# Two turns in a row, then the expert products of two tiles, with four places for their halves

## The reference, cut to what matters

```python
h = _swiglu(flat @ w1.T)
routed = jnp.zeros_like(shared)
for e in range(NUM_EXPERTS):
    routed = routed + h * w_se[:, e:e + 1] @ w2[e].T
return (shared + routed).reshape(Bs, Ts, C)
```

## Time and profile before

| | us |
|---|---|
| median of three executions | 1170.11 |
| lowest and highest | 1168.33, 1171.01 |
| the profiled execution | 1173.07 |
| its span, from the first to the last instruction | 1171.4 |
| TensorE busy in the span | 1107.7 (95%) |
| VectorE busy | 809.8 (69%) |
| GpSimd busy | 521.6 (45%) |
| ScalarE busy | 474.3 (40%) |

### The profile page before, as it was taken

How to read it: one execution, slowest core, us unless ns; L and a number is a source line. 1 busy time by engine, 2 the same in 40 slices (tenths; PEclk the granted TensorE clock), 3 DMA queues, 4 the chain that set the end, 5 groups by cost and what they waited for, 6 DMA issues and landing times.

```text
span 1171.4 us, 22483 instructions
## 1 busy us (share of the span) xinstructions
PE 1107.7 (95%) x7475; PEld 919.2 (78%) x7475; DVE 809.8 (69%) x1778; ACT 474.3 (40%) x723; POOL 521.6 (45%) x647
## 2 busy tenths in 40 slices
PE   3678999999999999999999899999999899999997
PEld 2456878887888788787787677788888788888886
DVE  6555687787686786876877676557554588777776
ACT  5454555555556545555555442223222111111111
POOL 6223446457447447356455522200000566666664
PEclk8887999999999999999999999999999899999999
DMA  8886566657647656665754411577662454545452
GB/s 154 219 135 125 114 107 134 131 92 148 137 103 126 131 119 102 144 131 114 125 118 88 90 40 43 172 243 257 213 207 100 150 159 152 164 159 155 152 162 73
DMA packets 106163, 160.65 MB, mean 137 GB/s; under 512 B 28828, under 2 KB 70718, under 8 KB 106048
## 3 DMA queue, kind: packets, MB, share of 16 engines
q1 hardware_dynamic: 94276, 121.18, 46.0%
q0 software_dynamic: 11776, 38.03, 10.5%
HBM read 75.24 MB, written 52.10 MB: 109 GB/s over the span
## 4 chain that ended last, share of the span: by engine, by line
PE 73%; DVE 8%; issue 8%; POOL 5%; DMA 3%; ACT 2%; SPq 1%; POOLq 0%; ACTq 0%; DVEq 0%
PE ps L744 15%; PE ps L791 11%; PE ps L689 9%; PE ps L706 6%; PE ps L793 6%; PE ps L609 4%; PE ps L597 4%; PE ps L640 3%; PE ps L776 3%; PE ps L565 2%; PE ps L569 2%; POOL tab_dram L1455 2%; DMA regr<-regr 1%; PE ps L592 1%; PE ps L663 1%
## 5 line engine op out<-in xcount | busy, mean ns | idle before, releaser
L791 PE MATMUL ps<-regr,gh 128*128 x600 | 222.1, 407 | 0.5 <-issue 0.3
L873 ACT ACTIVATE Pt<-ps,pbias 77x1024 f32<-77x1024 f32 x128 | 141.8, 1108 | 108.8 <-PE ps L597 104.8
L793 PE MATMUL ps<-regr,gl 128*128 x600 | 170.2, 284 | 0.0
L791 PEld LDWEIGHTS ps<-regr,gh 128*128 128x128 f32 x600 | 114.0, 190 | 24.4 <-issue 1.1
L963 ACT ACTIVATE gh<-ps 128x512 fp32r<-128x512 f32 x75 | 44.8, 600 | 206.9 <-PE ps L776 102.3
L1173 DVE TENSOR_REDUCE mneg<-ps 128x8 f32<-128x616 f32 x128 | 101.2, 792 | 29.7 <-PE ps L569 29.6
L793 PEld LDWEIGHTS ps<-regr,gl 128*128 128x128 f32 x600 | 114.2, 190 | 0.0
L689 PE MATMUL ps<-x2h,winh 128*128 128x512 f32 x256 | 110.2, 430 | 0.6 <-DVE OHR L1078 0.6
L1431 POOL TENSOR_TENSOR x<-x,regf 128x512 f32<-128x512 f32 x32 | 41.1, 1284 | 154.8 <-DMA x<-in_x 154.8
L1356 POOL TENSOR_TENSOR gl<-gf,gh 128x512 fp32r<-128x512 f32 x64 | 82.5, 1289 | 44.7 <-ACT gh L830 44.5
L689 PE MATMUL ps<-x2h,winl 128*128 128x512 f32 x256 | 101.5, 397 | 0.0
(11 more groups left out here) (202 smaller groups left out, 2678.9 us busy)
## 6 DMA issues: line engine op xcount, KB each, us to landing
regr<-regr SPq DMA_DIRECT2D x96, 256.0 KB, 5.9
y_dram<-Pt SPq DMA_DIRECT2D x64, 256.0 KB, 2.2
regf<-in_x SPq DMA_DIRECT2D x32, 256.0 KB, 3.0
x<-in_x SPq DMA_DIRECT2D x32, 256.0 KB, 7.2
y_dram<-res SPq DMA_DIRECT2D x32, 256.0 KB
regr<-regr SPq DMA_DIRECT2D x96, 77.0 KB, 6.9
x_dram<-x2h SPq DMA_DIRECT2D x14, 512.0 KB, 3.0
x_dram<-x2l SPq DMA_DIRECT2D x14, 512.0 KB, 3.8
```

The lines of the kernel that those rows point to most:

```text
L791: e.matmul(o, gh2[:, k % 3, fc, :], w2v[:, bass.ds(val, 1), fc, :, :].rearrange("p o h d -> p (o h) d"), start=fc == 0, stop=False, skip_g ...
L793: m = e.matmul(o[:, 0, :], gl2[:, k % 3, fc, :], w2v[:, bass.ds(val, 1), fc, 0, :].rearrange("p o d -> p (o d)"), start=False, stop=fc == ...
L873: e.activation(Pt[0:K, 4 * k:4 * k + 4, :].rearrange("k (n j) t -> k n (j t)", n=2), bank_of["sc", b, k][0:K, :, :], ACT.Exp, bias=pbias[: ...
```

## The change

`gh2` and `gl2` get four places instead of three (`k % 4`); ScalarE's wait for a free place moves by one tile with it. TensorE's list becomes turn(0), turn(1), experts(0), turn(2), and then for k = 1, 3, 5, ... 73: turn(k+2), turn(k+3), experts(k), experts(k+1), as far as there are tiles. VectorE's list follows: for odd k the halves of tiles k+2 and k+3 stand ahead of the accumulation of tile k, and for even k over 0 there are none ahead of it. SyncE and GpSimd have the lists and the waits they had. The lines behind L800 move down by one to four in the changed file: L963 is L964 there, L1280 is L1281, L1298 and L1301 are L1302 and L1305, L1342 and L1481 are L1346 and L1485.

```diff
-        gh2 = sb("gh2", [P, 3, 4, P], R)
-        gl2 = sb("gl2", [P, 3, 4, P], R)
+        gh2 = sb("gh2", [P, 4, 4, P], R)
+        gl2 = sb("gl2", [P, 4, 4, P], R)
...
             turn(0)
             turn(1)
-            for k in range(NTILE):
-                if k == 0:
-                    experts(k)
-                if k + 2 < NTILE:
-                    turn(k + 2)
-                if k:
-                    experts(k)
+            experts(0)
+            turn(2)
+
+            for k in range(1, NTILE, 2):
+                for n in range(k + 2, min(k + 4, NTILE)):
+                    turn(n)
+                experts(k)
+                experts(k + 1)
...
                 e.wait_ge(s["tz"], k + 1)
-                if k >= 3:
-                    e.wait_ge(s["ex"], 2 * (k - 2))
+                if k >= 4:
+                    e.wait_ge(s["ex"], 2 * (k - 3))
...
             for k in range(NTILE):
-                if k + 2 < NTILE:
-                    low_tile(k + 2)
+                if k == 0:
+                    low_tile(2)
+                elif k % 2:
+                    for n in range(k + 2, min(k + 4, NTILE)):
+                        low_tile(n)
```

More of the change, by code:

```diff
@@ L790, in experts @@
                     for fc in range(4):
-                        e.matmul(o, gh2[:, k % 3, fc, :], w2v[:, bass.ds(val, 1), fc, :, :].rearrange("p o h d -> p (o h) d"),
+                        e.matmul(o, gh2[:, k % 4, fc, :], w2v[:, bass.ds(val, 1), fc, :, :].rearrange("p o h d -> p (o h) d"),
                                  start=fc == 0, stop=False, skip_group_check=True)
-                        m = e.matmul(o[:, 0, :], gl2[:, k % 3, fc, :], w2v[:, bass.ds(val, 1), fc, 0, :].rearrange("p o d -> p (o d)"),
+                        m = e.matmul(o[:, 0, :], gl2[:, k % 4, fc, :], w2v[:, bass.ds(val, 1), fc, 0, :].rearrange("p o d -> p (o d)"),
                                      start=False, stop=fc == 3, skip_group_check=True)
@@ L960, in scalar @@
                 e.wait_ge(s["tz"], k + 1)
-                if k >= 3:
-                    e.wait_ge(s["ex"], 2 * (k - 2))
-                e.activation(gh2[:, k % 3, :, :], bank_of["tz", k, 0][:, :].rearrange("p (f t) -> p f t", f=4), ACT.Copy).then_inc(
+                if k >= 4:
+                    e.wait_ge(s["ex"], 2 * (k - 3))
+                e.activation(gh2[:, k % 4, :, :], bank_of["tz", k, 0][:, :].rearrange("p (f t) -> p f t", f=4), ACT.Copy).then_inc(
                     s["gh2"], 1)
@@ L1279, in low_tile @@
                 e.wait_ge(s["gh2"], k + 1)
-                e.tensor_tensor(gl2[:, k % 3, :, :], bank_of["tz", k, 0][:, :].rearrange("p (f t) -> p f t", f=4),
-                                gh2[:, k % 3, :, :].bitcast(F), ALU.subtract).then_inc(s["gl2"], 1)
+                e.tensor_tensor(gl2[:, k % 4, :, :], bank_of["tz", k, 0][:, :].rearrange("p (f t) -> p f t", f=4),
+                                gh2[:, k % 4, :, :].bitcast(F), ALU.subtract).then_inc(s["gl2"], 1)
             low_tile(0)
```

## The result

| | before | after |
|---|---|---|
| device time, median (us) | 1170.56 (1168.33 to 1172.03, 4 runs) | 1209.68 (1206.08 to 1214.68, 4 runs) |
| ratio, 95% interval | | 1.0341 (1.0312 to 1.0369) |
| profiled execution / its span (us) | 1173.07 / 1171.4 | 1207.88 / 1206.2 |
| first L791 of tile 0 to the last L793 (us) | 917.52 to 1164.02: 246.5 | 914.60 to 1198.83: 284.2 |

The kernel is 39 us slower by the medians, 3.4%. The two profiled executions differ by only 34.8 us of span, because in that of after the second phase happens to begin 2.9 us earlier (914.60 against 917.52).

The account below looks back on a forecast made before the run. TensorE bounds the stretch; late even-tile gathers were to make pairs 7.83 us: 938.05 + 33 x 7.83 = 1196.4, plus 12.2 gives 1208.7, 44.6 later than before, so 1214.7 us; range 1188 to 1238.

Parts of the forecast that it names:

- Part 1, the seam: On TensorE, two turns in a row save 0.01 us a pair over single turns, 0.3 us for 36 pairs.
- Part 2, four places: ScalarE's and VectorE's halves for a pair's second tile stay covered with some 0.9 us to spare; cost 0.
- Rival (d): Halves of the pair's second tile come late, a second wait: loop 8.5 or more, time over 1237; chance 0.10.
- Part 3, the gathers: Even tiles' turns move ahead of their GpSimd gathers' landing, so TensorE waits: loop 7.83 us a pair against 6.49.
- Turn to gather: From an even tile's turn on TensorE to the GpSimd gather its products release: 3.99 us, not 2.78.
- the 0.59: Unexplained part of tile 62's later release to GpSimd, taken into every pair's loop; without it the loop is 7.24.
- Issue to turn: From a gather's issue on GpSimd to its landing and the turn: 3.84 us, built from two rows.
- (a): The gather binds but TensorE's sequencer start costs nothing: loop 6.62, time 1174; chance 0.07.
- (b): Not slower: a gather lands within 3.1 us of its issue, the loop hides behind products, 1169.8; chance 0.06.
- (c): Each TensorE wait lets the clock fall for one tile of products: 85 us on top, some 1300; chance 0.05.
- the likeliest case: The forecast itself: a gather loop between 7.0 and 8.4 us a pair, 1187 to 1234; chance 0.72.

Follow-up runs that it names:

- after_early: The changed kernel with GpSimd's two waits for ex (scatter and gather) lowered by one tile: 1172.61 us, ratio 1.0017.
- before_early: The kernel before with GpSimd's two waits for ex (scatter and gather) lowered by one tile: 1171.32 us, ratio 1.0011.
- before_four: The kernel before, in its own order, with four places for the halves and ScalarE's wait one tile lower: 1169.90 us, ratio 1.0009.
- after_noload: The changed kernel without the load of the expert's number into TensorE's register, every tile using experts 0 and 1: 1193.33 us, ratio 1.0221.
- after_late: The changed kernel with the gather's wait for ex raised by one, to all products of tile m-5 instead of the first half: 1299.70 us, ratio 1.1094.

## Why the prediction came out as it did

**Part 1, the seam:** right. It was put at 0.01 us for a pair, and after_early against before_early shows none that counts: 214.11 against 214.28 us for the 33 pairs, 0.005 a pair.

**Part 2, four places:** right, 0. before_four and after_early show it from both sides. The reason given was wrong, though: in the new order both tiles of a pair are turned a whole pair ahead of their products, and none "just ahead of it". In after the halves of tile 10 are ready at 945.12, and its products start 9.2 us later:

```profile
944.43 0.69 DVE L1281 TENSOR_TENSOR gl<-ps,gh 128x512 fp32r<-128x512 f32 x1 [0.22 <-ACT gh L964]
...
954.29 0.40 PE L791 MATMUL ps<-regr,gh 128*128 x1
```

From tile 5 on no tile has less than 5.6 us of such cover, not the 0.9 that the prediction worked out. Rival (d), which grew from that reading, had no ground.

**Part 3, the gathers:** right in mechanism and place, too long in size. In every ordinary pair the turn of the even tile waits for its gather and L791 has its short gap behind it, as forecast; waits for the halves don't appear. Against the sum, counted from tile 0's first product:

| step | predicted (us) | measured (us) |
|---|---|---|
| first product to turn 8 | 938.05 - 917.52 = 20.5 | 935.65 - 914.60 = 21.1 |
| 33 pairs to turn 74 | 33 x 7.83 = 258.4 | 251.1 |
| turn 74 to the last L793 | 12.2 | 1198.83 - 1186.74 = 12.1 |

The last row is read from the end of the phase in after:

```profile
1186.74 0.63 PE L776 MATMUL ps<-ident,yt 128*128 128x128 f32 x4 [0.40 <-DMA yt<-y_dram,Pt]
...
1198.83 0.28 PE L793 MATMUL ps<-regr,gl 128*128 x1
```

The whole miss is in the loop, and within it in two terms. **Turn to gather** was put at 3.99, from the single case of tile 62 in before, and is 3.33. It consists of 2.78, the ordinary release, and 0.53 for the product's later start (0.88 against 0.35, forecast at 0.62); the 0.59 that the prediction took in, with "no reason for it beyond this row", does not recur in ordinary pairs. That was the term that was too long: one row in a disturbed place was made the state of all pairs, though the part that could be explained was already separated from the rest. Without it the prediction had 7.24. What delayed tile 62's release in before by 0.59 was not found, but it is not the mark of a turn that waited: in before the gathers of tiles 8 to 25 all start 2.78 behind the turn ahead of the products that release them, and those of tiles 26 to 74, the late one and all behind it, 2.80 to 5.17 (median 3.74), though only one turn there waits. In after GpSimd comes back to its rhythm behind each late gather. **Issue to turn** was put at 3.84, built of two rows, and is 4.06 by the median. Together 7.39. The 29 ordinary pairs took 7.41 on the mean, 0.42 less than forecast, which is 12.2 us in all. The four long pairs give back 4.9 us over 7.83 each, so that the miss is 7.3 in the loop. They were not in the prediction, although the late start at tile 62 could be seen in the earlier trace rows.

**The rivals.** (a) and (b) fell. From issue to turn it takes 4.06, and the landings that the trace has come 3.9 behind the issue by the median, not under 3.1; and the wait of some 0.3 us is enough to leave the sequencer empty: after_noload takes away just this half microsecond and 16 us of the time with it. (c) was the interesting one. In ordinary pairs, with eight transposes one behind the other and some 0.5 us of idle time, the granted clock stayed at 1.00 through 59 and 125 us. It fell to 0.50 behind the waits of 1.88 and 2.60 us in after, and behind 24 of those of some 1.6 us in after_late. The wait of tile 62 in before, 0.78 us, left it at 1.00, and so did the 1.72 us of tile 26 in after_noload and the three of 1.5 to 1.6 us in the window of after_late shown above, so that a wait of this length does not always bring it about. The Trainium skill (TensorE: Matmul & The Clock Gate, Part 4: PE-mode transpose) has the full clock not engage for transposes; the ordinary pairs here don't show that, since the granted clock was 1.00 through their transposes too.

**The range and the signs.** 1209.7 is 5 us under the forecast and inside the range and the likeliest case's own bounds. The four long pairs made the miss smaller than the loop alone would have; part of the agreement is therefore two errors of opposite sign.

## What to carry to other kernels

When a consumer is moved ahead, look for the producer whose release stays where it was: here an order on TensorE changed, and the loss was in two wait numbers on GpSimd that the diff doesn't touch. Write the loop from release to use and compare it with the work in between; when it comes out longer by a little, add what the waiting engine's sequencer has then not prepared. A size that comes from the one place where the old kernel already waited should be split into what is explained and what is not, and only the first multiplied by the number of rounds.

## What the runs showed of the hardware

- A register load on TensorE's sequencer, with the address worked out from it, is free while TensorE doesn't wait, and costs 0.5 us once it has waited for a semaphore: turn to product 0.88 with it, 0.39 without, no change of the time in the kernel that hardly waits (1.0000).
- Waits can cost more than their length: with waits of some 1.6 us a pair the granted clock was 0.50 in 24 stretches of 3.4 us and the time 1300 us; in the ordinary pairs of after, with waits of some 0.2 us, it stayed at 1.00.
- GpSimd's gather of tile 26 starts 1.6 us late in eleven of the twelve traces, also with 64 more instructions in GpSimd's list, and in the one run with 18 indirect DMAs put ahead the delay stands at tile 17. That of tile 62, 2.4 us, stays. The time is lost between the end of GpSimd's wait and its next instruction (2.14 and 2.93 in place of 0.54). The kernel before, with its slack, waits for neither by more than 0.78 us.
